# Projections beside a recurrence: a later place for the first copies, and up to four PSUM banks by turns

## What is computed

```python
def step(S, inp):                       # once per position, batch 2, 4 blocks
    logits_t, k_t, v_t, beta_t, q_t = inp
    ...
    delta = v_t - einsum('bnij,bnj->bni', S, kn)
    S_upd = tanh(beta_t[..., None] * S + outer(delta, kn))
    S_new = (1.0 - w) * S + w * S_upd
    ...
x = layernorm(x + L0_attn(x))           # the recurrence
x = layernorm(x + L0_xattn(x, ctx))
x = layernorm(x + L0_ffn(x))
x = layernorm(x + L1_attn(x))           # qkv = x @ W_qkv, softmax attention
x = layernorm(x + L1_xattn(x, ctx))
x = layernorm(x + L1_ffn(x))
```

## Time and profile before

| | |
|---|---|
| median of 3 runs | 2783.05 us (2777.99 to 2784.57) |
| profiled execution: time, span of its instructions | 2786.26 us, 2784.5 us |
| mean granted TensorE clock | 0.781 of full speed |
| busy over the span | DVE 80%, PE 74%, ACT 62%, POOL 23% |
| first and last copy of a chunk (L1346) | 471.4 and 1512.1 us from the span's start |
| idle time of ACT just before L1346 | 15.3 us in 12 cases, ended by PE's L1326 |

### The profile page before, as it was taken

One profiled execution on the slowest core, in us unless ns is written; L12 is line 12 of the kernel. 1 busy time (PEld: TensorE's weight loads), 2 busy tenths in 40 slices (PEclk: granted clock), 3 DMA queues, 4 the chain that ended last, 5 costly groups with the idle time before them and its releaser, 6 DMA issues. The chain is left out here.

```text
span 2784.5 us, 42524 instructions
## 1 busy us (share of the span) xinstructions
PE 2063.7 (74%) x11308; PEld 1210.6 (43%) x11308; DVE 2220.6 (80%) x10063; ACT 1731.5 (62%) x5762; POOL 654.1 (23%) x343
## 2 busy tenths in 40 slices
PE   6233555766666757667576769999999998799997
PEld 3122334454545544555445433333333332565654
DVE  5999999999999999999999846666666665186668
ACT  3578888888888888888888224444444444222231
POOL 0000000000000000000000027887787788000000
PEclk9655556576676676656757669999999999799998
DMA  4833222343343432333333011111111110201100
GB/s 110 166 100 66 51 56 67 70 115 81 81 104 82 116 83 71 102 81 100 88 70 87 5 38 31 56 45 40 45 34 51 34 49 12 88 12 43 46 8 8
DMA packets 154021, 180.27 MB, mean 65 GB/s; under 512 B 20916, under 2 KB 128344, under 8 KB 153816
## 3 DMA queue, kind: packets, MB, share of 16 engines
q1 hardware_dynamic: 153816, 178.00, 25.5%
HBM read 138.08 MB, written 39.88 MB: 64 GB/s over the span
## 5 line engine op out<-in xcount | busy, mean ns | idle before, releaser
L1595 ACT ACTIVATE mix_cand<-mix_pre,mixer_cbuf 128x32 f32<-128x32 f32 x2048 | 592.9, 289 | 151.0 <-DVE mix_pre L1521 75.6
L1592 ACT ACTIVATE mix_cand<-mix_state,mixer_cbuf 128x32 f32<-128x32 f32 x2048 | 653.8, 319 | 28.2 <-DVE mix_state L1513 4.7
L1508 DVE SCALAR_TENSOR_TENSOR mix_prod<-mixer_keys,mixer_cbuf,mix_cand 128x65 f32<-128x65 f32 x2048 | 580.0, 283 | 55.9 <-ACT mix_cand L1595 48.6
L1521 DVE SCALAR_TENSOR_TENSOR mix_pre<-mixer_keys,mix_gap,mix_state 128x32 f32<-128x32 f32 x2048 | 523.5, 256 | 27.7
L1513 DVE SCALAR_TENSOR_TENSOR mix_state<-mix_cand,mixer_cbuf 128x32 f32<-128x32 f32 x2048 | 504.2, 246 | 0.1
L2048 POOL TENSOR_TENSOR self_psum<-self_psum,self_prob 128x1024 f32<-128x1024 f32 x192 | 452.5, 2357 | 138.2 <-ACT self_prob L1970 130.2
L2062 DVE TENSOR_REDUCE self_tops<-self_rough 128x2 f32<-128x1024 f32 x252 | 307.5, 1220 | 202.7 <-PE self_rough L1844 196.6
L1626 PE MATMUL mix_out<-all_ident,mix_state 128*128 128x128 f32 x504 | 150.8, 397 | 415.3 <-ACT mix_flat L1575 372.0
L1970 ACT ACTIVATE self_prob<-self_sco 128x1024 f32<-128x1024 f32 x256 | 261.4, 1025 | 314.9 <-PE self_sco L1857 279.3
L876 POOL TENSOR_TENSOR mix_st_norm_rstd<-mix_st_norm_var,mix_half 128x2 f32<-128x2 f32 x24 | 17.4, 725 | 1323.4 <-DVE mix_st_norm_var L869 1323.4
L1626 PEld LDWEIGHTS mix_out<-all_ident,mix_state 128*128 128x128 f32 x504 | 78.3, 196 | 497.8 <-ACT mix_flat L1575 421.2
(11 more groups left out here) (395 smaller groups left out, 3466.9 us busy)
## 6 DMA issues: line engine op xcount, KB each, us to landing
mixer_keys<-k_rows SPq DMA_DIRECT2D x256, 260.0 KB, 5.1
mix_early_w<-in_w_qkv SPq DMA_DIRECT2D x48, 384.0 KB, 4.0
kq_rows<-mix_early_row SPq DMA_DIRECT2D x96, 128.0 KB, 2.1
self_qk<-kq_rows SPq DMA_DIRECT2D x16, 768.0 KB, 4.8
aT_rows<-self_aT SPq DMA_DIRECT2D x32, 256.0 KB, 2.7
two_aT<-aT_rows SPq DMA_DIRECT2D x8, 1024.0 KB, 6.8
v_rows<-mix_early_row SPq DMA_DIRECT2D x48, 128.0 KB, 1.8
self_v<-v_rows SPq DMA_DIRECT2D x16, 384.0 KB, 3.5
```

Source lines behind the costliest of these rows:

```text
L1508: dve.scalar_tensor_tensor(prod[:, b, :], keys[:, h, b, s_, :], coef(NIB, h, s_, b), cand[:, b, s % 2, :], ALU.mult, ALU.mult, accum_out=g ...
L1521: dve.scalar_tensor_tensor(pre[b], keys[:, h, b, s_, NS:2 * NS], gap[:, b:b + 1], state[:, hp, sp_, b, :], ALU.mult, ALU.add).then_inc(pre ...
L1592: act.activation(cand[:, b, (s + 1) % 2, NS:2 * NS], state[:, hp, sp_, b, :], ACT.Copy, scale=cbuf[:, h, KEEP, b, s_:s_ + 1]).then_inc(kep ...
L1595: act.activation(cand[:, b, (s + 1) % 2, 0:NS], pre[b], ACT.Tanh, scale=cbuf[:, h, BETA, b, s_:s_ + 1]).then_inc(c_ready[b], 1)
```

## The change

The table `WINDOWS` becomes `CHUNKS` (bank, place on PE, place on ACT) and `FREED` (a place on PE, and how many copies must have been made there). The first four copies of a round move from 17, 19, 21, 23 to 19, 21, 24, 26, while their products keep their places and now go to four banks, 0 to 3. The chunk at 35.2 is gone; the window from 74.6 has four chunks instead of five, with copies at 79, 81, 83, 86 instead of 77, 79, 81, 83, 86; the last window has 13 instead of 11, every two places from 89.6 to 113.6, in banks 2, 0, 1, 4 by turns, with copies 3.4 places behind, at 93, 95, 97 and so on to 117. A chunk now waits only until the chunk before it in its own bank has been copied. The DVE and POOL programs stay the same.

```diff
-    WINDOWS = ((33, ((2, 14.6, 17), (3, 16.6, 19), (2, 18.6, 21), (3, 20.6, 23), (2, 25.6, 28), (3, 27.6, 30), (2, 29.6, 33))),
-               (41, ((2, 35.2, 38),)),
-               (88, ((4, 74.6, 77), (3, 76.6, 79), (4, 78.6, 81), (3, 80.6, 83), (4, 83.6, 86))),
...
+    CHUNKS = ((0, 14.6, 19), (1, 16.6, 21), (2, 18.6, 24), (3, 20.6, 26), (2, 25.6, 28), (3, 27.6, 30), (2, 29.6, 33),
+              (4, 74.6, 79), (3, 76.6, 81), (4, 80.6, 83), (3, 82.6, 86),
...
+    FREED = ((22, 2), (33, 7), (88, 11), (114, 22), (117, 23), (119, 24))
...
-                if n > 1:
-
-                    pe.wait_ge(self.taken, n - 1)
...
+            of = [j for j in range(k) if self.CHUNKS[j][0] == bank]
+            if of:
+
+                pe.wait_ge(self.taken, i * self.N + of[-1] + 1)
...
+        for end in ends:
+            yield from self.freed(pe, i, end)
+
+    def freed(self, pe, i, end):
+
+        place, k = end
+        yield place
+        pe.wait_ge(self.taken, i * self.N + k)
```

48 lines of the change are left out of this document (22 added, 26 removed), and 4 rows, old and new, of tables (CHUNKS, WINDOWS).

## The result

| | before | changed |
|---|---|---|
| median of the first comparison, 7 runs each | 2783.05 us (2773.85 to 2787.29) | 2762.08 us (2760.25 to 2772.16) |
| profiled execution: time, span | 2786.26, 2784.5 us | 2760.35, 2758.6 us |
| mean granted TensorE clock | 0.781 | 0.784 |

The comparison was made twice more, on other chips, and did not agree with itself: 2762.41 us, ratio 0.9925 (0.9911 to 0.9938), and then 2772.70 us, ratio 0.9959 (0.9944 to 0.9973). The mean of 79 executions of before, in these and the other comparisons, is 2782.0 us.

The account below looks back on a forecast made before the run. DVE's own work sets the pace, so time is won only where DVE stands still. The terms 9.4 + 1.6 + 1.8 - 3.1 = 9.7 us, taken from the median 2783.05, gave 2773.4 us; 8-in-10 range 2767 to 2780.

Parts of the forecast that it names:

- Step 18: Round's first two chunks: later copies end ACT's 1.72 us wait, so DVE's 1.57 us go in each of six rounds, 9.4 us.
- Step 93: Copy moved one step later, past ACT's 0.83 us wait: 0.3 us a round, 1.8 us gained.
- Step 78: ACT still waits for the turned state, but the chunk copy behind it moves to step 79: 6 x 0.26 = 1.6 us gained.
- Step 117: Added cost: last chunk delays L1057 on PE; DVE stands 1.0 us at half clock, half of six rounds counted, 3.1 us lost.
- The count from the median: Profiled execution, 2786.26 us, taken as one of the longer ones, so the gain is subtracted from the median, 2783.05 us.
- edits that I cost at nothing: Chunk removed at 35.2, other moved copies, PE's new waits, later stores and weight loads: claimed to cost nothing.
- the clock's luck elsewhere: Allowance such as the 2.8 us at L1187, which may vanish or double; widens the range by 3 us each side.
- A: Rival: step 117 pays in every round, 6.2 us lost, gain 6.6, time 2776.5 us; chance 0.22.
- B: Rival: step 117 never pays because the clock is up each time; gain 12.8 us, time 2770.3 us; chance 0.20.
- C: Rival: waits only change their name, at the new copy place or steps 20 to 24; 2782.8 us; chance 0.06.
- D: Rival: weights late in the last window, at 97.6, 103.6 and 109.6, making it slower, up to 2793.2 us; chance 0.04.

## Why the forecast was wrong

By the averages of the traces (five of before, four of the change) the change takes 12.6 us off the steps and 4.3 off the rest, 16.9 together, where the executions' means differ by 16.3. From the forecast's 9.7 us to the 21.0 of the first comparison there are 11.3: 2.9 in the steps, 4.3 outside them, and 4.1 by which the medians of that comparison lie further apart than the average traces. Point by point:

- *Step 18: right.* 9.4 forecast, 9.6 measured, in every trace with the new places; the copy waits for nothing, and step 19, which now holds it, takes 0.06 us a round more.
- *Step 93: right in kind, a little low.* 1.8 forecast, 2.4 measured. The copy of the turned state did not wait in round 3, as PE's clock was up; the copies came cheap.
- *Step 78: right.* The copy behind the turn is gone and gives 0.27 us a round, 1.6 in six, as forecast. It can't be read from the step's length, since ACT's wait for the turn varies as well: against the profile shown the step is 4.0 us shorter, against the average of before 1.1.
- *Step 114: missed.* No term stood for it, because the profile shown had next to nothing to take there (7.89 us, with one wait of ACT of 0.2 us, which the forecast passed over as none). In the average of before it takes 9.67, in the change 7.77: 1.9 us. With step 78, with which it trades, the change saves 3.0 us against the forecast's 1.6: 1.6 by the copy and 1.4 by shorter waits.
- *Step 117: right in mechanism, too high in size.* A round that pays in full pays 1.23 us (2.76 less 1.53) and not 1.0, with DVE waiting 1.15. But only 10 of the 24 rounds in four traces pay, half of them in part, where half of all were put in full: 2.1 us and not 3.1. That the low clock makes them pay was right; in the five that pay in part it rises only under L1057 itself (0.80 to 0.93 there). They are rounds 2 and 3 in two executions, 6 and 7 in another and all four of these in the last, which agrees with the Trainium skill's rule (TensorE: Matmul & The Clock Gate, The HAM clock gate) that the stretches on which the clock is decided run free, though two of the four executions have the same rounds.
- *The count from the median: right.* The first trace of before was a long one, by L1187 (0 to 2 rounds in five traces) and by 1351.3 us outside the steps, where the others have 1345 to 1346.
- **The step that failed is the sum's edge.** It put the copy at step 113 among the "edits that I cost at nothing", because the one profile read had hardly a wait there, and everything outside the steps at nothing, and gave "the clock's luck elsewhere" 3 us to each side. That luck is larger: outside the steps, traces of all kernels lie between 1340.7 and 1351.3 us, in the steps those of one unchanged program between 1417.3 and 1423.2. The change's executions fall into two groups whose means are some 9 us apart. Two comparisons of three have their median in the lower one, beyond the range; the third gave 2772.7, near the forecast's 2773.4. That nearness is chance and no support for the sum, since the steps gain 2.9 us more than forecast.

The rivals. A (every round pays) and B (none pays) both fell; the price lies between. The second failure mode of the Trainium skill (the same page's section on PSUM-queue depth-cycling), by which the clock of a kernel that cycles through banks goes up and down and throughput is lost, was put beside A. It did not show: the mean clock is 0.784 against 0.781 (0.781 to 0.784 in four traces, 0.778 to 0.781 in five of before), 0.84 against 0.83 in steps 98 to 114, and 0.783 in two_banks, which has two banks where the change has four in the first window. C fell: no wait took the place of that at step 18. D fell: four waits of PE for weights, 0.4 us at most.

What stays open: whether the 4.3 us outside the steps belong to the change. Its four traces have 1341.1 to 1344.5 us and five of before 1344.9 to 1351.3, but other kernels with the same places in the first window have up to 1350.5. And it is not shown what decides which group an execution of the changed kernel falls into. In the first comparison the three long ones have the lower mean clocks (0.774 to 0.779, the four short ones 0.784 to 0.787), but the five long ones of the third have 0.778 to 0.783 and the five short ones of the second 0.781 to 0.784. Only one long execution was traced.

## What to carry to other kernels

Take from a trace, as a term of the sum, only what every round shows alike (step 18, step 93); a wait whose length goes with the granted clock can move to another step when it is taken away, as between 78 and 114 or from 117 to 115. Where such a wait varies, read the difference of two waits in the same round, which here was constant (step 78). Before such a kernel is forecast or judged, look at several traces of it, not one: a single profile hid a place that costs up to 3.7 us in six rounds and showed one that costs nothing in most executions. And repeat the comparison itself: one of three medians of the same program was 10 us from the other two.

## What the runs showed of the hardware

The executions of one unchanged program fell into two groups whose means are some 9 us apart. In the first comparison both appear, at mean granted clocks of 0.784 to 0.787 and of 0.774 to 0.779. A stretch in which DVE was the busiest engine took 59.8, 61.7 and 63.0 us for the same 53.9 us of DVE's work, at granted clocks of PE of 0.70, 0.67 and 0.62. A float32 product of 16 rows and 256 columns (L1057) took 2.07 us at the low clock and 1.13 at the high one. An extra product of a chunk's size on PE, beside an engine that sets the pace, cost nothing that could be measured (2763.1 us against 2762.1, 2762.4 and 2772.7), and it brought nothing either.
